# Three attention layers: one set of score banks for both batches, output products in their own banks, and row maxima in bfloat16 halves

## The reference

```
scores = einsum('bshd,bmhd->bhsm', qh, kh) / sqrt(hd)
probs  = softmax(scores, axis=-1)
out    = einsum('bhsm,bmhd->bshd', probs, vh)
```

## Time and profile before

| | us |
|---|---|
| median of 3 runs | 927.39 |
| lowest, highest | 922.25, 929.02 |
| the profiled execution | 923.17 |
| span of its instructions | 921.4 |
| mean granted PE clock | 0.969 |
| PE busy | 842.5 (91%) |
| DVE busy | 518.2 (56%) |
| ACT busy | 448.6 (49%) |

### The profile page before, as it was taken

One profiled execution on the slowest core, in us unless ns is written; L12 is line 12 of the kernel. 1 busy time (PEld: TensorE's weight loads), 2 busy tenths in 40 slices (PEclk: granted clock), 3 DMA queues, 4 the chain that ended last, 5 costly groups with the idle time before them and its releaser, 6 DMA issues.

```text
span 921.4 us, 10232 instructions
## 1 busy us (share of the span) xinstructions
PE 842.5 (91%) x4232; PEld 386.4 (42%) x4232; DVE 518.2 (56%) x708; ACT 448.6 (49%) x659; POOL 59.5 (6%) x44
## 2 busy tenths in 40 slices
PE   6988999699999999987899998999888989888987
PEld 2535444253434444553224334234455434544342
DVE  3479999733422012165735226369869595994442
ACT  3785222523345225344352543658865468752624
POOL 1000001320000000002100000000012000210000
PEclk9999999769999999997899999999989999999999
DMA  7000000100100000030000000000000000000011
GB/s 287 1 1 1 0 0 1 66 26 1 47 1 1 0 1 0 1 136 1 1 1 1 1 1 2 1 1 0 1 1 1 1 0 1 1 1 1 1 46 46
DMA packets 3005, 15.60 MB, mean 17 GB/s; under 512 B 657, under 2 KB 913, under 8 KB 2321
## 3 DMA queue, kind: packets, MB, share of 16 engines
q1 hardware_dynamic: 2816, 12.88, 3.6%
q0 software_dynamic: 144, 2.10, 0.5%
HBM read 12.87 MB, written 2.10 MB: 16 GB/s over the span
## 4 chain that ended last, share of the span: by engine, by line
PE 62%; DVE 19%; ACT 14%; issue 2%; DMA 2%; SPq 0%; POOL 0%; DVEq 0%; ACTq 0%
PE ps L419 60%; ACT AR L649 3%; DVE VB L665 3%; DVE AR L2045 3%; DVE AR L2042 3%; DVE AR L2041 2%; DMA WA<-in_m 2%; ACT AR L1893 2%; ACT AR L1883 1%; DVE AR L2192 1%; DVE VB L2045 1%; DVE WA L2045 1%; ACT AR L1590 1%; DVE AR L681 1%; ACT AR L1859 1%
## 5 line engine op out<-in xcount | busy, mean ns | idle before, releaser
L419 PE MATMUL ps<-AR,WA 128*128 128x512 f32 (+2 forms) x716 | 307.6, 594 | 6.9 <-DVE AR L2425 3.6
L419 PEld LDWEIGHTS ps<-AR,WA 128*128 128x128 f32 (+2 forms) x716 | 130.5, 188 | 172.5 <-issue 158.0
L419 PE MATMUL ps<-AR,CN 128*128 128x512 f32 (+3 forms) x304 | 103.5, 602 | 4.7 <-DVE AR L512 1.9
L419 PE MATMUL ps<-AR 128*64 128x128 f32 (+5 forms) x680 | 99.6, 416 | 8.5 <-ACT AR L1893 2.0
L681 DVE TENSOR_TENSOR AR<-ps,AR 128x512 f32<-128x512 f32 x24 | 16.6, 691 | 102.8 <-ACT AR L654 102.8
L419 PEld LDWEIGHTS ps<-AR 128*64 128x64 f32 (+4 forms) x680 | 52.4, 164 | 47.4 <-issue 22.0
L649 ACT ACTIVATE AR<-ps 77x2048 f32<-77x2048 f32 x24 | 43.9, 1868 | 43.9 <-PE ps L419 32.7
L665 DVE TENSOR_REDUCE VB<-ps 128x16 f32<-128x1232 f32 x32 | 44.9, 1438 | 35.8 <-PE ps L419 35.1
L419 PEld LDWEIGHTS ps<-AR,CN 128*128 128x128 f32 (+2 forms) x304 | 35.4, 158 | 51.7 <-issue 34.4
L1607 ACT ACTIVATE AR<-ps 128x512 f32<-128x512 f32 (+1 forms) x40 | 23.8, 596 | 62.6 <-DVE AR L2045 38.3
L419 PE MATMUL ps<-KB,WA 128*128 128x512 f32 (+1 forms) x120 | 53.1, 610 | 0.9 <-ACT AR L1876 0.9
(11 more groups left out here) (333 smaller groups left out, 1140.1 us busy)
## 6 DMA issues: line engine op xcount, KB each, us to landing
WA<-in_m SPq DMA_DIRECT2D x1, 2856.0 KB, 9.4
WA<-in_m SPq DMA_DIRECT2D x1, 2560.0 KB, 15.6
X<-in_xT POOLq DMA_DIRECT2D x1, 2048.0 KB, 9.3
WA<-in_m SPq DMA_DIRECT2D x1, 2048.0 KB, 7.2
out<-X SPq DMA_DIRECT2D x4, 512.0 KB, 3.1
WB<-in_m SPq DMA_DIRECT2D x1, 1024.0 KB, 4.7
AR<-in_rows SPq DMA_DIRECT2D x1, 640.0 KB, 10.0
WA<-in_m SPq DMA_DIRECT2D x1, 512.0 KB, 16.4
```

Source lines behind the costliest of these rows:

```text
L419: return nc.tensor.matmul(out, lhsT, rhs, start=first, stop=last)
```

## The change

- The loop runs over items in the order (g, b, k). All items use banks 0 to 3 for their scores, so the scores of item n + 1 wait for the exponential of item n. They are issued ahead of the weighing of item n.
- The weighing writes bank 4 + 2b (values) and 5 + 2b (sums); with `pairs=1`, bank 4 and 5 for both batches, and then a batch's weighing waits for the L681 of the batch before. The sums are done first and have a semaphore of their own, for which the logarithm waits. `pairs=1` is used for a2, j = 1 and a3, j = 0, whose hung-in matmuls now use banks 6 and 7.
- The hung-in work is tied to items; the mean squares of a3, j = 0 come after the loop.
- The maxima go to a float32 tile MXF. After the last set of a batch DVE makes a bfloat16 copy of it and the difference to it, also bfloat16, side by side in MXP (two small instructions for each batch). The transpose is a bfloat16 matmul with an identity, MXT is bfloat16, and the selecting weight adds both halves in one bfloat16 pass.
- 66 columns of constants are added (34 KB to the transfer of CN), and some semaphores are shared.

```diff
-    MXP = [VB[:, b * 1024:b * 1024 + T].rearrange("p (s n) -> p s n", s=SUB) for b in range(B)]
-    MXT = [VB[:, b * 1024 + T:b * 1024 + 2 * T] for b in range(B)]
+    MXP = [VB[:, b * 1024:b * 1024 + T // 2].bitcast(BF16).rearrange("p (s n) -> p s n", s=SUB) for b in range(B)]
+    MXT = [VB[:, b * 1024 + T // 2:b * 1024 + T].bitcast(BF16) for b in range(B)]
+    MXF = [VB[:, b * 1024 + T:b * 1024 + T + SUB * 16].rearrange("p (s r n) -> p s r n", s=SUB, r=4) for b in range(B)]
+    ID16 = cn("ident16").bitcast(BF16)
+    SEL16 = cn("sel16").bitcast(BF16)
...
-            pe.wait_ge(*after("att_mx", nset(p, j, len(sets) - 1, b)))
+            pe.wait_ge(*after("att_mp", nunit(p, j, b)))
             for s in range(SUB):
-                last = nc.tensor.transpose(bank(b, 0)[:, s * P:(s + 1) * P], MXP[b][:, s, :], cn("ident"))
+                last = mm(bank(b, 0)[:, s * P:(s + 1) * P], MXP[b][:, s, :], ID16)
             last.then_inc(sem("att_mt"), 1)
 
-    def attn_pe(pe, p, j, masked=False, qs=QS, ready=None, meanwhile=None, begun=False):
-        sets = key_sets(p)
+    def attn_items(p):
+
+        return [(g, b, k) for g in range(DC) for b in BS for k in range(PARTS[p])]
+
+    def out_bank(b, pairs, to):
+
+        return ps[:, 4 + 2 * (b % pairs) + to, :]
+
+    def attn_pe(pe, p, j, masked=False, qs=QS, meanwhile=None, begun=False, pairs=2):
         if not begun:
             maxima_pe(pe, p, j, masked, qs)
...
+        sets, items = key_sets(p), attn_items(p)
+
+        def scores(n):
+            g, b, k = items[n]
+            if g == 0 and k == 0:
+                pe.wait_ge(*after("att_mc", nunit(p, j, b)))
+            if n:
+                pe.wait_ge(*after("att_ex", nitem(p, j, *items[n - 1])))
+            i = sets.index((g, k))
+            for r in range(4):
+                row = slice(32 * r, 32 * r + 32)
+                mm(bank(0, r)[0:M, :], KF[row, k, g, b, :], qs[b][row, g, :], True, False)
+            for r in range(4):
+                row = slice(32 * r, 32 * r + 32)
+                last = mm(bank(0, r)[0:M, :], SEL16[row, i:i + 1].broadcast_to([32, M]), MXT[b][row, :], False, True)
+            last.then_inc(sem("att_p2"), 1)
+
+        def weighed(n):
+            g, b, k = items[n]
+            pe.wait_ge(*after("att_ex", nitem(p, j, g, b, k)))
+            if (g, b, k) == (0, 0, 0):
+                pe.wait_ge(*after("att_mc", nunit(p, j, B - 1)))
+            elif k == 0 and g * B + b >= pairs:
+                pe.wait_ge(*after("att_ctx", CHUNKS[p] + nk(j, DC * B, g * B + b - pairs)))
+            for to in (1, 0):
+                for r in range(4):
+                    head = slice(g * P + 32 * r, g * P + 32 * r + 32)
+                    lhsT = ONEP[p][k] if to else VS[:, k, b, head]
+                    last = mm(out_bank(b, pairs, to)[32 * r:32 * r + 32, :], lhsT, PTX[b][:, k, r, :], k == 0, k == PARTS[p] - 1)
+                if k == PARTS[p] - 1:
+                    last.then_inc(sem("att_den" if to else "att_pv"), 1)
+
+        scores(0)
+        for n, (g, b, k) in enumerate(items):
+            if n + 1 < len(items):
+                scores(n + 1)
+            weighed(n)
+            if meanwhile:
+                meanwhile(g, b, k)
-    def attn_act(act, p, j, bias=0.0, table=True, meanwhile=None):
+        sets, items = key_sets(p), attn_items(p)
+
+        def scores(n):
+            g, b, k = items[n]
+            if g == 0 and k == 0:
+                pe.wait_ge(*after("att_mc", nunit(p, j, b)))
+            if n:
+                pe.wait_ge(*after("att_ex", nitem(p, j, *items[n - 1])))
+            i = sets.index((g, k))
+            for r in range(4):
+                row = slice(32 * r, 32 * r + 32)
+                mm(bank(0, r)[0:M, :], KF[row, k, g, b, :], qs[b][row, g, :], True, False)
+            for r in range(4):
+                row = slice(32 * r, 32 * r + 32)
+                last = mm(bank(0, r)[0:M, :], SEL16[row, i:i + 1].broadcast_to([32, M]), MXT[b][row, :], False, True)
+            last.then_inc(sem("att_p2"), 1)
+
+        def weighed(n):
+            g, b, k = items[n]
+            pe.wait_ge(*after("att_ex", nitem(p, j, g, b, k)))
+            if (g, b, k) == (0, 0, 0):
+                pe.wait_ge(*after("att_mc", nunit(p, j, B - 1)))
+            elif k == 0 and g * B + b >= pairs:
+                pe.wait_ge(*after("att_ctx", CHUNKS[p] + nk(j, DC * B, g * B + b - pairs)))
+            for to in (1, 0):
+                for r in range(4):
+                    head = slice(g * P + 32 * r, g * P + 32 * r + 32)
+                    lhsT = ONEP[p][k] if to else VS[:, k, b, head]
+                    last = mm(out_bank(b, pairs, to)[32 * r:32 * r + 32, :], lhsT, PTX[b][:, k, r, :], k == 0, k == PARTS[p] - 1)
+                if k == PARTS[p] - 1:
+                    last.then_inc(sem("att_den" if to else "att_pv"), 1)
+
+        scores(0)
+        for n, (g, b, k) in enumerate(items):
+            if n + 1 < len(items):
+                scores(n + 1)
+            weighed(n)
+            if meanwhile:
+                meanwhile(g, b, k)
+
+    def attn_act(act, p, j, bias=0.0, table=True, meanwhile=None, pairs=2):
         if table:
             nc.scalar.preload_act_table_set("natural_log_exp_and_others")
+
+        def inverse(g, b):
+            act.wait_ge(*after("att_den", nchunk(p, j, g, b)))
+            nc.scalar.activation(RTB[b], out_bank(b, pairs, 1), ACT.Ln).then_inc(sem("att_ln"), 1)
+            act.wait_ge(*after("att_ln", nchunk(p, j, g, b)))
+            nc.scalar.activation(RTB[b], RTB[b], ACT.Exp, scale=-1.0).then_inc(sem("att_r"), 1)
+            if meanwhile:
+                meanwhile(g, b)
+
+        items = attn_items(p)
+        for n, (g, b, k) in enumerate(items):
+            act.wait_ge(*after("att_p2", nitem(p, j, g, b, k)))
+            nc.scalar.activation(PTX[b][:, k], ps[0:M, 0:4, :], ACT.Exp, bias=bias).then_inc(sem("att_ex"), 1)
+            if k == 0 and n:
+                inverse(*items[n - 1][:2])
+        inverse(*items[-1][:2])
+    def maxima_dve(dve, p, j, second=None):
         sets = key_sets(p)
...
+        for i, (g, k) in enumerate(sets):
             for b in BS:
                 if second and (i, b) == (1, 1):
                     second()
                 dve.wait_ge(*after("att_p1", nset(p, j, i, b)))
-                where = MXP[b].rearrange("p s (r n) -> p r s n", n=32)
+                where = MXF[b].rearrange("p s r n -> p r s n")
                 nc.vector.tensor_reduce(where[:, :, :, i] if PARTS[p] == 1 else where[:, :, 2 * k:2 * k + 2, 2 * g:2 * g + 2],
                                         ps[:, 4 * b:4 * b + 4, 0:HALF].rearrange("p r (s m) -> p r s m", m=M), AX.X, ALU.max, negate=True).then_inc(sem("att_mx"), 1)
+                if i == len(sets) - 1:
+                    parts = MXP[b].rearrange("p s (r n) -> p s r n", n=32)
+                    exact, upper, lower = MXF[b][:, :, :, 0:i + 1], parts[:, :, :, 0:i + 1], parts[:, :, :, 4:5 + i]
+                    dve.wait_ge(*after("att_mx", nset(p, j, i, b)))
+                    nc.vector.tensor_copy(upper, exact).then_inc(sem("att_mh"), 1)
+                    dve.wait_ge(*after("att_mh", nunit(p, j, b)))
+                    nc.vector.tensor_tensor(lower, exact, upper, ALU.subtract).then_inc(sem("att_mp"), 1)
         for b in BS:
             dve.wait_ge(*after("att_mt", nunit(p, j, b)))
             nc.vector.tensor_copy(MXT[b], bank(b, 0)).then_inc(sem("att_mc"), 1)
 
-    def attn_dve(dve, p, j, meanwhile=None, first=None, then=None, begun=False):
+    def attn_dve(dve, p, j, meanwhile=None, then=None, begun=False, pairs=2):
         if not begun:
             maxima_dve(dve, p, j)
         if meanwhile:
             meanwhile()
         for g in range(DC):
-            if first and g == 0:
-                first()
             for b in BS:
                 dve.wait_ge(*after("att_r", nchunk(p, j, g, b)))
-                nc.vector.tensor_tensor(ST[b][:, g, :], bank(b, 0), RTB[b], ALU.mult).then_inc(sem("att_ctx"), 1)
-            if then and g == 0:
-                then()
+                dve.wait_ge(*after("att_pv", nchunk(p, j, g, b)))
+                nc.vector.tensor_tensor(ST[b][:, g, :], out_bank(b, pairs, 0), RTB[b], ALU.mult).then_inc(sem("att_ctx"), 1)
+                if then:
+                    then(g, b)
...
+        def first_squares(g, b, k):
+            if (g, b, k) == (0, 0, 1):
+                for u in BS:
+                    pe.wait_ge(*after("norm_sqs", NORMS["x3"] + u + 1))
+                    mm(bank(1, 2 + u), cn("mean"), SQ2[u][:, 0, :]).then_inc(sem("norm_ms"), 1)
+            elif (g, b, k) == (1, 1, 0):
                 pe.wait_ge(*after("norm_ln", NORMS["x3"] + B))
+                for u in BS:
+                    pe.wait_ge(*after("ra_sqs", u + 1))
+                    mm(bank(1, 2 + u), cn("mean"), SQA[u][:, 0, :]).then_inc(sem("ra_ms"), 1)
...
```

(54 more changed lines are left out.)

103 lines of the change are left out of this document (17 added, 86 removed).

## The result

The changed kernel takes **951.96 us** (median of 4 runs, 949.69 to 955.82) against 927.62 (922.25 to 929.02, 4 runs) before: a ratio of 1.028, with a 95% interval from 1.026 to 1.031. It is slower, by 24 us. The forecast was 933.0 in a range of 925.0 to 941.5, and the time lies above it; 0.21 had been given to slower by over 1%. The profiled execution lasted 953.9 us, 30.7 more than the one of before.

A forecast was written before the change was run, and what follows sets the result against it. PE was taken to bound the kernel, the loops changing to a chain through the exponential. Loops +0.1, maxima +5.1, constants +0.1, clock -1.0 or +1.6 gave +4.3 or +6.9; median 927.4 + 5.6 = 933.0 us, range 925.0 to 941.5.

The forecast's parts named there:

- The chain: In the loops: scores 1.39, exponential 1.87 and hand-over 0.06 bound each item at 3.32 us (3.41 in a3).
- The select: In the scores: four bfloat16 selecting matmuls take 0.23 us, not 0.86, saving 0.63 us of PE in each of 32 items.
- The maxima: After each batch's last reduction: a copy and a subtraction on the chain, 0.50 to 0.55 us a pair, +5.1 us in sum.
- its own terms, 2.2, 2.0 and 0.8: Costs of the small DVE operations: a2 pays 1.1 and a3 1.0, each twice; a0, j = 1 pays 0.8 us.
- The hung-in work: In the loops with pairs=1: waits and extra matmuls make a2, j = 1 +0.4 us and a3, j = 0 +1.8 us.
- The clock: In a0, j = 0: -1.0 us if 2.4 GHz comes back in time, +1.6 us if only after more PE work.
- hidden: In the maxima: the bfloat16 transposes lie behind the COPY, so they were given no term in the sum.
- the worse of the two cases: In a0, j = 0: the clock returns only after PE has again run scores and a weighing; the loop takes 1.6 us more.
- The first rival's case: In a0, j = 0: the clock stays at 1.2 GHz through the loop, +13.7 us in all, 941 us; 15%.
- The rival that named the clock in the loops: In the loops: 0.4 us gaps make the clock fall again, eight items of 32 cost another 20 us, 953 us; 4%.
- The other rival at 953: In the scores: the bfloat16 pass gains nothing, the chain is 3.95 us, 20 us more, 953 us; 4%.
- The median: Whole kernel before: the median of the runs, 927.4 us, is 4.2 above the profiled execution, which was on the lucky side.

The follow-up runs named there:

- both spares: Changed kernel plus unread float32 matmuls between the two batches' transposes and behind the first scores of each attention: 930.2 us, ratio 1.004.
- banks alone: Changed kernel with float32 maxima, transposes and select as before, no small DVE operations; one set of score banks stays: 952.4 us, ratio 1.031.
- no pairs: Kernel before, two sets of banks, with reductions writing bfloat16 maxima directly in one part, bfloat16 transposes and select, no small DVE operations: 921.6 us, ratio 0.994.
- the maxima alone: Kernel before with only the maxima in bfloat16 halves, including the small DVE operations; two sets of score banks and old order stay: 924.8 us, ratio 1.000.
- spares behind the scores: Changed kernel plus unread float32 matmuls only behind the first scores, none between the transposes: 941.5 us, ratio 1.017.
- with the transposes filled: Changed kernel plus unread float32 matmuls only between the transposes of batch 0 and batch 1: 944.5 us, ratio 1.019.

## Why the prediction was wrong

- **The chain: right.** 3.28 us an item against 3.32. With the clock held, the four loops that forecast and table can compare at full clock came to 16.58, 28.29, 34.25 and 15.46 against 16.9, 28.4, 34.6 and 15.6.
- **The select: right.** The group behind four bfloat16 matmuls starts 0.32 us after them (513.83 to 514.15 above), where I took 0.23 (it is 0.22 where scores follow, 249.64 to 249.86 in the kernel before without pairs); but the exponential starts 0.44 after them (543.26 to 543.70 in the changed kernel), where I took 0.47, and that is the link of the chain.
- **The maxima: right in place, a little low.** 12 pairs at 0.49 make 5.9 us; the forecast was +5.1 (its own terms, 2.2, 2.0 and 0.8, add to 5.0), with the two in a0, j = 0 at nothing. The operations took 0.18 to 0.20 and 0.19 to 0.23.
- **The hung-in work: right in kind.** PE waits 1.07 and 0.65 us in a2, j = 1 and 2.27 in a3, j = 0. The latter loop is 24.2 to 24.9 us even with both spares, forecast 21.7: behind the same wait of 2.27 the clock falls there too (at about 872 with the pairs), and the mean squares and first output matmuls run at 1.2 GHz.
- **The clock: the step that failed.** The forecast asked for the clock in a0, j = 0 only, "PE's pause of 2 us after the first scores is what decides", and gave the other five loops the 1.00 of the earlier trace rows. But the same pause stands at the head of every loop, and ahead of it the pause between the transposes, which my own pairs made longer (0.69 to 1.44 us) while I had the shorter bfloat16 transposes down as "hidden". I priced the work there and not what its absence does. The traces show this pause, for which the forecast has no term, as the one that begins the fall, and the pause of 2 us as what draws it out. All six loops ran below 1.00, 158.3 us against the forecast's 133.8 or 136.4, and filling both pauses gave back 22 of the 26 us (1.0283 to 1.0041). In a0, j = 0 the worse of the two cases came, and a little more: 2.2 us longer, forecast 1.6. The first rival's case, half the clock through all of that loop, did not: 2.4 GHz is back at about 210.4, 7 us before its end.
- **The rival that named the clock in the loops** had 4% and 953 us, and hit the time for a reason not its own: by its terms the falls come from the gaps of 0.4 us in every item. Those gaps, 0.1 to 0.2 us of idle time in the trace, keep the clock (exponentials at 540.42 to 550.26 at an even 3.28 us). The Trainium skill ("TensorE: Matmul & The Clock Gate", section "A second HAM failure mode: psum-queue depth-cycling") says that short idle times between groups of matmuls, from cycling through banks, make the clock fall and rise again. This case agrees that it falls and comes back, in most loops once (141 us at 1.2 GHz in all), but not with the gaps between items as the cause. The other rival at 953, a bfloat16 pass that gains nothing, came near the time by chance too: the pass takes 0.32 us and not 0.86.
- **The median** was taken to lie 4.2 above the profiled execution "perhaps in this very clock". The clock it is, though the record doesn't say in which part of the span: over the 58 executions of the kernel before that were timed beside the experiments, those with a mean clock of 0.969 or more took 921.4 to 926.5 us, those with 0.963 or less 927.4 to 929.7. The profiled one had 0.969.

What stays open: why the clock is lost behind a wait in some loops and not in others. Between the transposes, 0.69 and 0.95 us kept it at the head of a2 and a3 (kernel before, banks alone, no pairs), and 1.40 to 1.44 mostly lost it, but not in a3, j = 0 of the maxima alone, nor in a3, j = 1 with spares behind the scores. Behind the first scores, a2, j = 0 kept it at 1.97 us with the transposes filled, a0, j = 1 lost it at 2.38 with two sets of banks. And in three of the profiled executions (either spare alone, and the maxima alone) it fell already at the start of the maxima of a2, j = 0, behind waits of 0.8 and 1.04 us that stand in the other kernels too without a fall. No run varied one pause in small steps with all else left alone.

And the scheme itself: with the pairs gone and spares in place, one set of banks has a ratio of 0.998 (0.996 to 1.000) and two sets 0.993 (0.990 to 0.996); the intervals just meet, so this rests on the loops too. With the same maxima all the loops that keep their clock are shorter with two sets: 14.62, 28.04, 32.69 and 14.80 us against 15.09, 28.29, 34.25 and 15.46. The gain of this study is in the bfloat16 maxima written directly; in no run did the shared banks add to it.

## What to carry to other kernels

Where a change turns a loop from bound by PE to bound by a chain, price the pauses that PE gets, not only where PE's work goes: read the granted clock at the head of the loop, where fill-in waits stand close together, and expect a fall to cost more than the pause (here 4 to 5 us in each of five loops, 158.3 against 134.6 in sum). A cheap test is to put matmuls nobody reads into the pause; if the time falls, it was the clock. And write a reduced value in the type that the next engine wants, rather than convert it on the path.
